# A two-layer cross-attention and mixture-of-experts kernel: new attention core with two-term fp32r stacks and key-tile exponentials

## What is computed

```python
def xattn(queries, keys, Wq, bq, Wk, bk, Wv, bv, Wo, bo):   # heads 8, hd 4 (layer 0); heads 16, hd 16 (layer 1)
    q = split_heads(queries @ Wq + bq)
    k = split_heads(keys @ Wk + bk)
    v = split_heads(keys @ Wv + bv)
    attn = softmax(einsum('bhqd,bhkd->bhqk', q, k) * scale)
    o = einsum('bhqk,bhkd->bhqd', attn, v)
    return merge_heads(o) @ Wo + bo

x = x + xattn(layernorm(x), ctx, layer 0)
x = x + experts(x, E=8, top 2, hidden 1024)
x = x + xattn(layernorm(x), ctx, layer 1)
x = x + experts(x, E=15, top 3, hidden 256) + shared expert
```

## Time and profile before

| | us |
|---|---|
| runs | 1612.24, 1610.02, 1605.36 |
| median | 1610.02 |
| span of the profiled execution | 1607.1 |
| mean granted TensorE clock in it | 0.856 |

### The profile page before, as it was taken

The page is one execution under the profiler, slowest core; times in us unless marked ns, Lnnn a source line. Parts: engine busy times, 40 slices in busy tenths (PEclk is TensorE's granted clock), DMA queues, the critical chain, the costliest instruction groups (busy, mean ns, idle before and its releaser), DMA issues. The chain is left out here.

```text
span 1607.1 us, 20254 instructions
## 1 busy us (share of the span) xinstructions
PE 1256.6 (78%) x6250; PEld 810.2 (50%) x6251; DVE 788.3 (49%) x1610; ACT 549.8 (34%) x1053; POOL 376.1 (23%) x370
## 2 busy tenths in 40 slices
PE   7559983617999999997847999998861899999910
PEld 5202343507999999995421333336730455555500
DVE  0558717425555566644167888842430113444423
ACT  1407640314434444430132666661230102233200
POOL 3010003773222233304230000000037000111156
PEclk9859986567999999996575999998786899999965
DMA  4264310343322223204132222105412202222234
GB/s 107 80 220 140 131 37 18 101 159 128 112 83 95 92 71 107 96 17 133 28 107 77 60 61 60 59 8 176 160 50 104 102 0 73 84 82 82 71 88 136
DMA packets 110635, 144.43 MB, mean 90 GB/s; under 512 B 26618, under 2 KB 90464, under 8 KB 108902
## 3 DMA queue, kind: packets, MB, share of 16 engines
q1 hardware_dynamic: 98038, 101.62, 20.2%
q0 software_dynamic: 12528, 41.94, 7.6%
HBM read 95.10 MB, written 48.76 MB: 90 GB/s over the span
## 5 line engine op out<-in xcount | busy, mean ns | idle before, releaser
L682 DVE TENSOR_REDUCE M<-S 128x1 f32<-128x512 f32 x384 | 248.7, 685 | 71.4 <-PE S L534 67.7
L659 ACT ACTIVATE PT<-S 128x1024 f32<-128x1024 f32 x192 | 196.1, 1025 | 103.0 <-PE S L553 102.8
L534 PE MATMUL S<-KS,QS 96*128 96x512 bf16 x384 | 162.2, 427 | 47.1 <-DMA KS<-scrk 20.5
L534 PEld LDWEIGHTS S<-KS,QS 96*128 96x128 bf16 x384 | 38.7, 101 | 188.9 <-DVE M L682 139.0
L1044 POOL TENSOR_TENSOR w12l<-stage,w12h 128x1024 fp32r<-128x1024 f32 x32 | 77.5, 2425 | 202.6 <-ACT w12h L1038 202.5
L1620 PE MATMUL H<-W,XST 128*128 x248 | 121.8, 614 | 2.1 <-issue 0.9
L553 PE MATMUL S<-QS,KS 98*128 98x512 bf16 x384 | 117.0, 389 | 8.0 <-DMA QS<-NM 5.0
L1220 DVE TENSOR_TENSOR HTm0l<-HFm,HTm0h 128x320 fp32r<-128x320 f32 x128 | 122.3, 956 | 1.0
L565 PE MATMUL PV<-PT,VG 128*32 128x512 f32 x768 | 101.9, 608 | 7.8 <-ACT OSB L640 7.8
L1226 DVE TENSOR_TENSOR HFm<-Um,SGm 128x320 f32<-128x320 f32 x128 | 62.3, 486 | 78.9 <-ACT SGm L1189 78.5
L521 POOL COPY VG<-VA 128x512 f32<-128x512 f32 (+1 forms) x24 | 14.7, 613 | 362.2 <-PE PV L565 334.0
(11 more groups left out here) (240 smaller groups left out, 2491.1 us busy)
## 6 DMA issues: line engine op xcount, KB each, us to landing
stage<-in_W12T SPq DMA_DIRECT2D x32, 512.0 KB, 6.1
xs<-zeros POOLq DMA_DIRECT2D x12, 1024.0 KB, 7.3
QS<-scrq SPq DMA_DIRECT2D x144, 64.0 KB, 2.2
KS<-scrk SPq DMA_DIRECT2D x144, 64.0 KB, 2.3
stage<-in_W3T SPq DMA_DIRECT2D x16, 512.0 KB, 3.9
XS<-xs SPq DMA_DIRECT2D x62, 128.0 KB, 2.0
ys<-YS POOLq DMA_DIRECT2D x62, 128.0 KB, 2.0
W<-in_fc1T SPq DMA_DIRECT2D x2, 3840.0 KB, 22.2
```

The costliest lines, as they stand in the source:

```text
L534: pe.matmul(S1[:, q % 2, :], QS[0:ROWS, slot, h, q * P:(q + 1) * P], KS[0:ROWS, slot, h, :], start=True, stop=True).then_inc(s1_ready, 1)
L659: act.activation(PT[:, c % 2, h, 2 * u:2 * u + 2, :], S2[:, u, :, :], ACT.Exp, scale=lay.scale).then_inc(exp_done, 1)
L682: dve.tensor_reduce(M[:, c % 2, h * TPB + q:h * TPB + q + 1], S1[:, q % 2, :], AX.X, ALU.max).then_inc(max_done, 1)
```

## The change

- **Stacks.** q and k are split into two fp32r terms instead of three bfloat16 ones, and three products are summed (q terms 0, 0, 1 with k terms 0, 1, 0). A head takes 3 x hd rows (48 in layer 1, 12 in layer 0) and two more for the maximum. Two heads lie in one stack, one in partitions 0 to 63, one in 64 to 127 (`ROWQ`). No head is padded. A group's stacks are loaded by four DMAs; a unit is stored by three, one for each term of the product (three times 256 KB in layer 1). The scratch is float32.
- **Maxima.** One reduction takes two heads: 128x2x512 to two columns, from two banks; 8 for each group. 14 of them stand ahead of the first scores. POOL negates and splits the result, TensorE transposes it, ACT copies it, and two DMAs put it into the stack.
- **Scores and exponentials** go by key tile: for each of four key tiles, four scores (one for each head) and four exponentials of 512; values of a key tile follow its own exponentials by one tile, and are read from `VA` without a copy on POOL.
- **Normalisation** is token-major: `OSB` is transposed (L528), and DVE inverts the sums and multiplies into `OT`. Columns, widening and spreading are gone.
- **Output projection**: `OT` is transposed (`turn_output`, `keep_output`) into `ONT`, and one matmul (layer 0) or two (layer 1) serve a token tile.
- **Biases**: the bias matmul of V is gone; bv times Wo plus bo is formed once in `project` (`BO`) and added to X by POOL during the attention.
- **project**: weights come by one DMA each; X is loaded ahead of the last three context parts; the memset of KS is 128x4096 float32 at the start of POOL's list instead of 32x8192 bfloat16 at its end; `Wo` is loaded here. `fill_slots` issues two zero fills a group, each time after the maxima of the group before.

```diff
-Q_TERMS = (0, 0, 0, 1, 1, 2)
-K_TERMS = (0, 1, 2, 0, 1, 0)
+ROWQ = 64
+TERMS = {"q": (0, 0, 1), "k": (0, 1, 0)}
...
+    def second(self, dve, i):
+        dve.wait_ge(self.p1_done, i + 1)
+        dve.scalar_tensor_tensor(self.parts[0:U, i % PB, 1, :], self.pq[0:U, i % 2, :],
+                                 self.bias[w][:, half:half + 1], self.parts[0:U, i % PB, 0, :].bitcast(F32),
+                                 ALU.add, ALU.subtract).then_inc(self.p2_done, 1)
...
+        for n, part in enumerate(TERMS[w]):
+            sp.dma_start(dst[n], self.parts[0:U, i % PB, part, :].bitcast(F32)).then_inc(self.stored[i % PB], 16)
...
-            pool.wait_ge(env.wo_zero, 1)
-            pool.memset(st.KS[ROWS:ROWS + 32, :, :, :], 1.0).then_inc(st.shift_ones, 1)
+            pool.memset(st.KS[:, :, :, :].bitcast(F32), 1.0).then_inc(st.ones_done, 1)
...
-                pe.matmul(pv[:, t % 2, 0:width], env.ones[0:1, :], bv[:, :],
-                          start=False, stop=True).then_inc(v_ready, 1)
...
+            def maxima(g, u):
+                for j in range(2):
+                    r = ROWQ * j
+                    m = pe.matmul(S1[:, n % 2, j, :], QS[r:r + RM, slot, h, q * P:(q + 1) * P], KS[r:r + RM, slot, h, :],
+                                  start=True, stop=True)
...
+            for g in range(NG):
+                for kt in range(TPB):
+                    for i in range(2):
+                        scores(g, kt, i)
+                    if kt == 0:
+                        if g + 1 < NG:
+                            maxima(g + 1, 6)
+                        if g:
+                            values(g - 1, TPB - 1)
+                    else:
+                        if g + 2 < NG:
+                            maxima(g + 2, 2 * kt - 2)
+                        values(g, kt - 1)
+                    for i in range(2, 4):
+                        scores(g, kt, i)
...
+                dve.tensor_reduce(M[:, g % 2, :, h, q], S1[:, n % 2, :, :], AX.X, ALU.max).then_inc(max_done, 1)
```

More of the change, by code:

```diff
@@ L207, in remain @@
         w, half, b = self.units[i]
+        U = self.lay.rows
         dve.wait_ge(self.p1_done, i + 1)
[L209 to L216, removed]
@@ L318, in _ @@
                     gather(pool, env, experts, YG, added, n)
-            pool.wait_ge(env.wo_zero, 1)
-            pool.memset(st.KS[ROWS:ROWS + 32, :, :, :], 1.0).then_inc(st.shift_ones, 1)
-            pool.wait_ge(st.shift_ones, 1)
+            pool.wait_ge(w_loaded["v"], 32)
+            for f in range(halves):
+                pool.tensor_scalar(BVB[:, f, :], env.ones[0:U, :], bias["v"][:, f:f + 1], None, ALU.mult).then_inc(bvb_done, 1)
         @block.vector
@@ L382, in _ @@
                 for half in range(halves):
-                    i = n_k + b * halves + half
-                    split.first(act, i)
-                    if i > n_k:
-                        split.second(act, i - 1)
-            split.second(act, len(units) - 1)
+                    split.first(act, n_k + b * halves + half)
+            act.wait_ge(bo_ready, 1)
+            act.copy(env.BO[:, :], pb[:, 0:D])
         @block.tensor
         def _(pe):
-            pe.wait_ge(w_loaded["v"], weights["v"])
+            pe.wait_ge(w_loaded["v"], 32)
             for t in range(NT):
@@ L424, in _ @@
                     split.product(pe, n_k + b * halves + half, XNT)
+            pe.wait_ge(env.wo_loaded, 32)
+            pe.wait_ge(bvb_done, halves)
+            for f in range(halves):
+                pe.matmul(pb[:, 0:D], BVB[:, f, :], env.WO[0:U, f, :], start=(f == 0), stop=False)
+            pe.matmul(pb[:, 0:D], env.ones[0:1, :], bo[:, :], start=False, stop=True).then_inc(bo_ready, 1)
 class Stacks:
@@ L668, in _, with negate, keep @@
-            steps(act, step)
-            for m in range(NG - 2, NG):
-                keep(*divmod(m, SLOTS))
-                widen(*divmod(m, SLOTS))
+            def negate(g):
+                act.wait_ge(mt_ready, g + 1)
+                if g >= 2:
+                    act.wait_ge(nm_loaded[(g - 2) % SLOTS], 32 * ((g - 2) // SLOTS + 1))
+                act.copy(NM[:, g % 2, :], MISC[0:32, 0:P]).then_inc(nm_done, 1)
+            def keep(g):
+                act.wait_ge(pv_done, TPB * (g + 1))
+                if g:
+                    act.wait_ge(ot_ready, g)
+                act.copy(OSB[:, :], PV[:, :]).then_inc(osb_done, 1)
@@ L719, in _, with maxima @@
-            steps(dve, step)
-            normalize(*divmod(NG - 3, SLOTS))
-            for m in range(NG - 2, NG):
-                invert(*divmod(m, SLOTS))
-                normalize(*divmod(m, SLOTS))
+            def maxima(g, u):
+                h, q = divmod(u, TPB)
+                n = g * UNITS + u
+                if u == 0 and g >= 2:
+                    dve.wait_ge(mh_done, g - 1)
+                dve.wait_ge(s1_ready, n + 1)
+                dve.tensor_reduce(M[:, g % 2, :, h, q], S1[:, n % 2, :, :], AX.X, ALU.max).then_inc(max_done, 1)
@@ new lines, in _ @@
+            for u in range(UNITS):
+                maxima(0, u)
+            for u in range(6):
+                maxima(1, u)
+            for g in range(NG):
+                for kt in range(TPB):
+                    if kt == 0:
+                        if g + 1 < NG:
+                            maxima(g + 1, 6)
+                            maxima(g + 1, 7)
+                    else:
+                        if kt == 3 and g:
+                            normalize(g - 1)
+                        if g + 2 < NG:
+                            maxima(g + 2, 2 * kt - 2)
+                            maxima(g + 2, 2 * kt - 1)
```

571 lines of the change are left out of this document (238 added, 333 removed).

## The result

Against sixteen runs of the kernel before, median 1612.4 us, the changed kernel took 1.0056 times as long, with a 95% interval of 1.0036 to 1.0076; in the profiled execution the span is 1615.3 us where it was 1607.1. So it is slower by about 9 us, where 1565 us and a gain of 45 had been forecast. The sixteen runs of the changed kernel spread from 1616 to 1665 us (median 1627.0), those of before only from 1604 to 1616; the ratio is taken over its nine lower runs, up to 1627, and the experiments show where the spread comes from.

A forecast was written before the change was run, and what follows sets the result against it. Attention was taken as bound by a ring of scores, exponential and values in TensorE's order, not one full engine. Terms -15 + 20 - 6 + 2 - 25 - 13 - 8 = -45 on 1607.1 gave 1562, forecast 1565 us, range 1545 to 1590.

The forecast's parts named there:

- First projection, -15: First projection: no bias matmuls, X loaded earlier, fewer terms and loads; some 3 us wait for X; -15 us.
- Which clock: Both attentions: half clock in the first (+20 us), full in the second with some drops (+5 us, within its -13).
- rival B: Both attentions at full clock: -43 us in the first, 1522 us in all; chance 0.27.
- rival C: Second attention at half clock too: +88 us less 5 of drops, 1648 us in all; chance 0.10.
- The ring at half clock, 19.2: First attention's steady loop of scores, exponentials and values: 4.64 us per key tile, 19.2 per group at half clock.
- First output projection and K stores, -6 + 2: First router stage: fewer output matmuls less added transposes and copies, -6 us; doubled second-layer K stores, +2 us.
- Second projection, -25: Second projection: value tiles without bias matmuls reach ACT's root sooner, and a shorter stretch to the attention; -25 us.
- -19.5 for the value tiles: Second projection: 16 value tiles at 2.08 instead of 3.30 us, passed on to ACT's root, DVE and the 25th gather.
- The 14.6 us from the 25th gather to that copy: Second projection: time from the 25th gather (802) to the last stretch's first normalised copy (816.6), forecast to stay.
- Second attention, -13: Second attention at full clock, 13.5 us per group, with 5 us for drops: 239.7 against 252.5 us, -13.
- Second output projection, -8: Second output projection: two matmuls per tile instead of four, less added transposes and ACT copies; -8 us.
- Rival D: Both attentions: the two 64-row stacks don't run side by side, each pair 0.43 us for 0.22; 1611 us; chance 0.12.

The follow-up runs named there:

- the fuller rows: Changed kernel with scores of both layers on 62 and 64 rows of each stack, added query rows zero: ratio 0.9709 to the kernel before, median 1567.7 us.
- the edit of the stores: Layer 1's scratch reshaped so each 256 KB store writes 128 rows in one stretch: 0.9969 on the changed kernel; 0.9573, 1546.2 us with 62 and 64 rows.
- that of the copies: DVE instead of ACT copies the second projection's value tiles, added to 62 and 64 rows and reshaped stores: ratio 0.9520, median 1537.6 us.
- the three edits: Changed kernel with 62 and 64 score rows, reshaped layer 1 stores and value copies on DVE together: ratio 0.9520 to the kernel before, median 1537.6 us.

## Why the prediction was wrong

The sum came to -45 and the traces to +8; the two steps that cost most are the price of the stores and the value tiles of the second projection. In the order of the terms:

**First projection, -15: right** (-15.8). The wait for the context behind X was 5.3 us, not 3.

**Which clock: half right.** The step that took half clock for the first attention from the value projection's one-row matmuls held, and rival B fell with it. The Trainium skill, "TensorE: Matmul & The Clock Gate" (Part 1), has the level follow how busy the PE has been; the traces disagree, with 99.7% busy at 0.53 and 85% at 0.97. "Full for the second, with some drops" was right for the profiled run, but the sentence that its stacks use "96 of the rows in pairs, as many as today" missed that such pairs do not hold the clock reliably: 0.92, 0.50 and 0.99 came in turn with 48 and 50 rows. In its runs of 1641 to 1665 us the changed kernel is rival C in part: up to 50 us above its lowest run, where C had 83 for a whole attention at half clock, since the clock does rise at some time. That the profiled run had the early rise is luck.

**The ring at half clock, 19.2: too low by 1.4 us a group** (20.63). Sum 4.64 for a key tile, measured 4.98: from the third score's start to the exponential it was 153.82 - 152.99 = 0.83 and not 0.65, since a pair of scores took 0.79 and not 0.60, and from the end of these two exponentials (153.82 + 1.08 = 154.90) to the next values (156.11) it was 1.21 and not 1.01. Six groups make 8.6 us of the missing 11, and the last two with the tail 2.3 (39.8 for 37.5). At full clock 13.8 for 13.5: two exponentials take 1.08, but the values begin 0.65 us after the score before them, not 0.53.

**First output projection and K stores, -6 + 2: wrong**, +9.4. Up to DVE's first read of the router's logits the stage gained 3.2 us (66.2 to 63.0), with TensorE at half clock all along; then the stores took 12.6. The step that failed is "before, 384 KB took 2.5 us": I took the rate of the old stores for the new ones. The new ones write 8 blocks of 16 rows, and with these the engines were half busy at 203 GB/s; the edit that makes one block of 128 rows gave some 380 GB/s and 15 us in this stage. The range of 0 to +5 came from an old shape, and a DMA of a new shape has no old row.

**Second projection, -25: wrong**, -5.9. The step that failed is that ACT's root follows the value tiles as fast as TensorE makes them. -19.5 for the value tiles was -14.1 at the root: TensorE could even run at full clock, 0.87 us a tile and not 2.08, but ACT's copies stood still for 21.7 us in sum beside the gathers. That the two errors nearly cancel in this term is luck. The trace of before has such a stall of 7.5 us, which ends at 774.7 and was left out of the sum. The 14.6 us from the 25th gather to that copy stayed, as forecast. The stretch to the attention rose by 8.2 us and did not fall by 5, by the stores again.

**Second attention, -13: too much by 7**, from 0.3 us a group, a stay at half clock of 7 us at the start and one drop near 1000. **Second output projection, -8:** -6.9.

Rival D fell: the pair takes 0.50 us. The Trainium skill, "TensorEngine Tiling (Array Packing)" (Key Properties), says that tiles work in parallel, and the trace agrees.

So of 53 us between forecast and result, 12 lie in the first attention (9 of them in the ring at half clock), 7 in the second attention, 13 in the first router stage and 19 in the second projection; on top of the fuller rows, the edit of the stores gave 21 us back and that of the copies 9.

## What to carry to other kernels

Packing a contraction into fewer rows can cost the clock: look at the rows that the matmuls occupy in the stretches of the trace at either level, before and after, and if the new number is below all that held the full clock, fill the rows so that their products are zero, which cost one hidden memset here. Price a DMA by a row of the same shape, not of the same size; if the engines stand at exactly half while only it runs, try it as one block of rows. And when an engine stands still with its input ready beside another engine's indirect DMAs, count on more of it once the engine in front gets faster; which engine stands still can change. With the three edits the new attention core is 4.8% faster than the kernel before, and the clock was the greater part of it.

## What the runs showed of the hardware

- In the steady parts of these attentions the granted clock went by the rows that the score matmuls use, and not by the busy share. One stack of 32 to 34 or 64 to 66 rows: 0.53 at 99.7% busy. Two stacks of 12 to 14 or 24 to 26 rows each: 0.50 at 95 and 96% busy. Two of 48 to 50: either level. Two of 62 to 64: 0.97 at 85% busy; one of 96 to 98: 1.00 at 96%. Rows alone don't decide it either: in the starts of both attentions of the kernel before, with 96 rows and TensorE busy 56 and 78%, it was 0.50. Rows whose products are zero count: zeros against ones in the filled stacks, and zeros against zeros in layer 0 of the kernel before (12 of 16 rows of every term).
- Stores of 256 KB as 8 blocks of 16 rows ran at 203 GB/s with the DMA engines half busy; as one block of 128 rows at some 380 GB/s with all of them busy.
- ACT's copies stood still four times, for 1.8 to 8.7 us, while POOL's indirect gathers were in flight, and not at all when they were not. DVE's copies in the same place did not, but DVE had a stall of 6.6 us beside the last gathers in the experiment that issues them late. Why is open.
